# A chain of six transformer blocks on one core: value and output weights multiplied once, gates of all batches ahead of the loop, and a shifted residual moved tile by tile

## What is computed

```python
q = rms_norm(x @ Wq.T) * qk_gain ; k = rms_norm(x @ Wk.T) ; v = x @ Wv.T      # per head
g = sigmoid(x @ Wg.T + bg)                                  # per row and head
attn = softmax(where(mask, q @ k.T / sqrt(128), -inf))      # within a chunk of 64
y_in = attn @ v
gamma = exp(sum(log(g) over the chunk))
yc = q @ state ; state = state * gamma + k.T @ v            # from chunk to chunk
y = (y_in + yc) @ Wo.T
```

```python
def shift_token(t):
    t1, t2 = split(t, 2, axis=-1)
    t2 = pad(t2, ((0, 0), (1, 0), (0, 0)))[:, :-1]          # the row before
    return concatenate([t1, t2], axis=-1)
x = x + o @ wo
h = layer_norm(shift_token(x)) ; a, g = split(h @ w1 + b1, 2)
x = x + (a * gelu(g)) @ w2 + b2
```

## Time and profile before

| what | value |
|---|---|
| median of 3 runs | 2083.44 us (2080.21 to 2089.17) |
| profiled execution, its own time | 2075.68 us |
| its span | 2073.5 us |
| TensorE busy | 80% of the span |
| VectorE / ScalarE / GpSimd busy | 60% / 53% / 41% |
| mean granted TensorE clock | 0.899 |
| linear attention | 0 to 353 us |
| windows, first stage | 353 to 787 us |

### The profile page before, as it was taken

The page is one execution under the profiler, slowest core; times in us unless marked ns, Lnnn a source line. Parts: engine busy times, 40 slices in busy tenths (PEclk is TensorE's granted clock), DMA queues, the critical chain, the costliest instruction groups (busy, mean ns, idle before and its releaser), DMA issues. The chain is left out here.

```text
span 2073.5 us, 38265 instructions
## 1 busy us (share of the span) xinstructions
PE 1665.5 (80%) x13589; PEld 1193.2 (58%) x13589; DVE 1240.1 (60%) x3682; ACT 1090.7 (53%) x2758; POOL 854.6 (41%) x630
## 2 busy tenths in 40 slices
PE   6999998789998955888887789998856746858685
PEld 5888886466666633334544466666644535647464
DVE  2554543787777724555773787777726874545554
ACT  3656664677778722566543677888722102324232
POOL 1322322776666511223443866666504660321002
PEclk9999999999999986999876999999978877969888
DMA  4000000011111100000000111111100000000001
GB/s 193 1 1 1 1 1 1 22 29 30 24 28 29 27 5 1 1 1 2 1 2 1 27 24 29 25 29 31 25 6 0 1 1 0 21 21 1 1 6 56
DMA packets 31082, 36.55 MB, mean 18 GB/s; under 512 B 19120, under 2 KB 21168, under 8 KB 30512
## 3 DMA queue, kind: packets, MB, share of 16 engines
q1 hardware_dynamic: 29872, 32.01, 5.9%
q0 software_dynamic: 1024, 2.10, 0.3%
HBM read 12.08 MB, written 3.15 MB: 7 GB/s over the span
## 5 line engine op out<-in xcount | busy, mean ns | idle before, releaser
L965 ACT ACTIVATE arena<-ps 128x512 f32<-128x512 f32 (+4 forms) x702 | 377.1, 595 | 305.0 <-PE ps L321 122.8
L1200 ACT ACTIVATE arena<-ps 128x320 f32<-128x320 f32 (+4 forms) x256 | 132.2, 561 | 133.0 <-PE ps L679 130.6
L1100 ACT ACTIVATE arena<-arena,g_small 128x128 f32<-128x128 f32 x512 | 199.1, 404 | 0.5
L1550 DVE CUSTOM_DVE_ANT_0 arena<-ps,consts,g_ss 128x128 f32<-128x128 f32 x512 | 145.5, 346 | 78.9 <-PE ps L485 77.3
L321 PE MATMUL ps<-consts,arena 128*128 128x128 f32 x400 | 82.1, 351 | 136.8 <-DVE arena L1433 60.4
L2079 POOL TENSOR_TENSOR arena<-arena,consts 128x512 f32<-128x512 f32 (+1 forms) x64 | 93.5, 1461 | 191.2 <-ACT arena L1200 191.2
L2100 POOL TENSOR_TENSOR arena<-arena 128x512 f32<-128x512 f32 x64 | 82.2, 1284 | 181.7 <-DVE arena L1558 181.7
L321 PEld LDWEIGHTS ps<-consts,arena 128*128 128x128 f32 x400 | 57.8, 178 | 166.9 <-DVE arena L1433 65.4
L679 PE MATMUL ps<-arena 32*128 32x160 f32 (+4 forms) x1024 | 119.8, 461 | 21.3 <-ACT arena L1200 10.8
L1557 DVE TENSOR_TENSOR arena<-ps,tabs 128x512 f32<-128x512 f32 x128 | 87.6, 685 | 51.5 <-ACT arena L1069 44.8
L679 PEld LDWEIGHTS ps<-arena 32*128 32x128 f32 x1024 | 60.8, 210 | 87.4 <-ACT arena L1200 55.3
(11 more groups left out here) (253 smaller groups left out, 4262.3 us busy)
## 6 DMA issues: line engine op xcount, KB each, us to landing
arena<-arena SPq DMA_DIRECT2D x112, 128.0 KB, 2.3
weights<-in_w SPq DMA_DIRECT2D x1, 5069.0 KB, 24.2
weights<-in_w SPq DMA_DIRECT2D x1, 2052.0 KB, 12.7
arena<-Y SPq DMA_DIRECT2D x16, 128.0 KB
arena<-Y SPq DMA_DIRECT2D x16, 127.0 KB
consts<-in_c SPq DMA_DIRECT2D x1, 1278.0 KB, 8.8
out<-X SPq DMA_DIRECT2D x1, 1024.0 KB, 5.1
sorted_rows<-arena,e_idx POOLq DMA_INDIRECT x32
```

The costliest lines, as they stand in the source:

```text
L965: copy = lambda o, i: act.activation(o, i, ACT.Copy)
L1100: last = act.activation(g_p[:, n % 2, 4 * hf + i, :], g_sc[:, 4 * hf + i, :], ACT.Exp, scale=-1.0, bias=g_mn[:, h:h + 1], accum_out=g_rs[: ...
L1200: act.activation(b_p[:, U % 2, 2 * gp:2 * gp + 2, at:at + n], ps[:, b:b + 2, 0:n], ACT.Exp, scale=float(HD) ** -0.5).then_inc(s.b_exp, 1)
L1550: last = dve.tensor_tensor_reduce(g_sc[:, 4 * hf + i, :], ps[:, 4 + hf, i * P:(i + 1) * P], C("mask_f" if n % NT else "mask_f0"), g_ss[:, ...
```

## The change

It has four parts.

1. Since `(P v) Wo = P (x (Wv Wo))`, the value weights and output weights of each head are multiplied once (`fold_weights`, in two halves of four heads, by way of banks 3 and 4). `project_v` then makes values that already hold the output projection; `mix` is 10 matmuls of 128x128 with the probabilities stationary and adds up 8 heads in bank 6. `out_rows` and `keep_y` are gone, and `add_rows` reads bank 6.
2. `project_v` writes bank 7 and waits only for its own previous copy; `turn_q` waits for `a_kT` in place of `a_vin`.
3. x of all four batches is normalised and turned at the start; gates and decays are made once for all batches. The decay sums are three matmuls and six small adds on VectorE (`spans`), on which `turned_scores(0)` waits.
4. `shift` runs for each tile: two DMAs, and a third for the one row that passes to the next tile, behind `lookback` in SyncE's loop. 176 increments a group in place of 48 stand in the two waits on `gs.sh`.

```diff
+                def fold_weights(half):                      # TensorE
+                    for k in range(4):
+                        h = 4 * half + k
+                        last = tr(ps[:, 3, k * P:(k + 1) * P], W("a_qkv", 2048 + h * P, 2048 + (h + 1) * P), ident)
+                    last.then_inc(s.a_wT_ps, 1)
+                    pe.wait_ge(s.a_wT, half + 1)
+                    need(pe, s.a_vo, half)
+                    for k in range(4):
+                        h = 4 * half + k
+                        last = mm(ps[:, 4, k * P:(k + 1) * P], a_wT[:, k, :], W("a_wo", h * P, (h + 1) * P),
+                                  start=True, stop=True)
+                    last.then_inc(s.a_vo_ps, 1)
...
+                def gates():
+                    pe.wait_ge(s.a_xT, NB)
+                    for i in range(TT):
+                        last = mm(ps[:, 5, i * HA:(i + 1) * HA], a_xT[:, i // NT, i % NT * P:(i % NT + 1) * P], W("a_wg"),
...
+                def decays():
+                    pe.wait_ge(s.a_decay, 1)
+                    for k, name in enumerate(("half0", "ones", "cross")):
+                        last = mm(ps[:, 5, P * k + P:P * k + 2 * P], C(name), a_gate, start=True, stop=True)
                     last.then_inc(s.a_gsum, 1)
...
                 def project_v(n):
-                    need(pe, s.a_kT, n)
+                    need(pe, s.a_vin, n)
+                    pe.wait_ge(s.a_vo, h // 4 + 1)
                     for j in range(NT):
-                        last = mm(ps[:, 2, j * P:(j + 1) * P], a_xT[:, z % 2, j * P:(j + 1) * P],
-                                  W("a_qkv", 2048 + h * P, 2048 + (h + 1) * P), start=True, stop=True)
+                        last = mm(ps[:, 7, j * P:(j + 1) * P], a_xT[:, z, j * P:(j + 1) * P],
+                                  a_vo[:, h, :], start=True, stop=True)
...
                 def turned_scores(n):
                     need(pe, s.a_cross, n)
+                    if n == 0:
+                        pe.wait_ge(s.a_spans, 1)
...
                 def mix(n):
-                    need(pe, s.a_yT, n)
-                    pe.wait_ge(s.a_xT, begun(n, -4))
-                    pe.wait_ge(s.a_gate_in, begun(n, -3))
-                    pe.wait_ge(s.a_gamma, begun(n, -2))
-                    for i in range(NT):
-                        last = mm(ps[:, 6, i * P:], a_v[:, n % 4, i, :], a_mt[:, n % 2, i, 0:(NT - i) * P],
-                                  start=i == 0, stop=i == NT - 1, skip_group_check=True)
+                    if h == 0:
+                        need(pe, s.a_add, z)
+                    for i in range(NT):
+                        for j in range(i, NT):
+                            last = mm(ps[:, 6, j * P:(j + 1) * P], a_mt[:, n % 2, i, (j - i) * P:(j - i + 1) * P],
+                                      a_v[:, n % 4, i, :], start=h == i == j == 0, stop=h == HA - 1,
+                                      skip_group_check=True)
...
-                    if head(t - 1):
-                        out_rows(t - 1)
+                    if t == -4:
+                        turn_x(0)
+                    if t == -2:
+                        for z in range(1, NB):
+                            turn_x(z)
+                        gates()
+                    if -3 <= t < -1:
+                        fold_weights(t + 3)
                     if head(t + 2):
                         project_v(t + 2)
-                    if begins(t, -4):
-                        turn_x(t)
-                    if begins(t, -3):
-                        gates(t)
-                    if begins(t, -2):
-                        decays(t)
+                    if t == -1:
+                        decays()
```

ScalarE's loop, VectorE's start and its decay sums, and SyncE's loop:

```diff
                 for t in range(-4, HEADS + 1):               # ScalarE
-                    if begins(t, -1):
-                        decays(t)
+                    if t == -4:
+                        keep_x(0)
                     if head(t):
                         exps(t)
                         keep_raw(t)
-                    if head(t - 1):
-                        keep_y(t - 1)
                     if head(t + 1):
                         keep_q(t + 1)
+                    if t == -2:
+                        for z in range(1, NB):
+                            keep_x(z)
                     if head(t + 2):
                         squares(t + 2)
...
+                    if -3 <= t < -1:
+                        fold_weights(t + 3)
+                    if t == -2:
+                        log_gates()
...
+                    if t == -1:
+                        decays()
...
+                def spans():                                 # VectorE
+                    dve.wait_ge(s.a_gsum, 1)
+                    halves, tiles, over = (ps[:, 5, P * k:P * k + P].rearrange("p (z j h) -> p j z h", z=NB, j=NT)
+                                           for k in (1, 2, 3))
+                    after(dve.tensor_copy(a_dec[:, 0], over[:, 0:3]))
+                    tt(a_dec[:, 1], a_dec[:, 0], halves[:, 1:4], ALU.add)
...
+                for z in range(NB):
+                    variance(z)
+                for z in range(NB):
+                    norm_x(z)
...
+                def shift(n):                                # SyncE
+                    N, i, j = n0 + n, n % TT, n % NT
+                    sp.wait_ge(gs.add, N + 1)
+                    need(sp, gs.h2, m0 + n // NT)
+                    sp.dma_start(g_h[1:P, j, 64:128], Y[0:P - 1, i, 64:128]).then_inc(gs.sh, 16)
+                    sp.dma_start(g_h[:, j, 0:64], Y[:, i, 0:64]).then_inc(gs.sh, 16)
+                    if j < NT - 1:
+                        sp.dma_start(g_h[0:1, j + 1, 64:128], Y[P - 1:P, i, 64:128]).then_inc(gs.sh, 16)
...
-                    if at_step(t, 5):
-                        shift((t - 5) // 4)
                     if live(t + 2):
                         lookback(t + 2)
+                    if live(t - 2):
+                        shift(t - 2)
```

More of the change, by code:

```diff
@@ L366, in project_qk @@
                         for j in range(NT):
[L367 removed]
+                            last = mm(ps[:, c, j * P:(j + 1) * P], a_xT[:, z, j * P:(j + 1) * P],
                                       W("a_qkv", 1024 * c + h * P, 1024 * c + (h + 1) * P), start=True, stop=True)
@@ L967, in linear_attention, with keep_x, log_gates, decays @@
             def linear_attention():
-                def keep_x(t):
-                    z = (t + 4) // HA
+                def keep_x(z):
                     act.wait_ge(s.a_xT_ps, z + 1)
[L972 to L987, removed]
+                    copy(a_xT[:, z, :], ps[:, 7 - z % 2, :]).then_inc(s.a_xT, 1)
+                def log_gates():
+                    act.wait_ge(s.a_gate_in, 1)
+                    after(act.activation(a_gate, a_gate, ACT.Exp, scale=-1.0))
+                    act.activation(a_gate, a_gate, ACT.Ln, bias=1.0).then_inc(s.a_decay, 1)
+                def decays():
+                    act.wait_ge(s.a_spans, 1)
+                    for k, n in ((0, 3), (2, 2), (4, 1)):
+                        v = a_dec[:, k:k + 2, 0:n].rearrange("p k i z h -> p k (i z h)")
+                        last = act.activation(v, v, ACT.Exp, scale=-1.0)
+                    last.then_inc(s.a_gamma, 1)
                 def exps(n):
@@ L1438, in linear_attention, with variance @@
                 stream = lambda z: X[:, NT * z:NT * z + NT, :]
[L1440 to L1447 removed]
+                def variance(z):
+                    for i in range(NT * z, NT * z + NT):
+                        last = dve.bn_stats(stats[:, i, :], X[:, i, :])
+                    after(last)
+                    for i in range(NT * z, NT * z + NT):
+                        last = dve.bn_aggr(mv[:, i, :], stats[:, i, :])
+                    after(last)
+                    ts(rstd[:, NT * z:NT * z + NT], mv[:, NT * z:NT * z + NT, 1], EPS5, None, ALU.add).then_inc(gs.var, 1)
+                    rooted.next()
@@ new lines, in norm_x, with add_gate_bias @@
+                def norm_x(z):
+                    dve.wait_ge(gs.root4, z + 1)
+                    for i in range(NT * z, NT * z + NT):
+                        last = ts(Y[:, i, :], X[:, i, :], mv[:, i, 0:1], rstd[:, i:i + 1], ALU.subtract, ALU.mult)
+                    last.then_inc(gs.ln, 1)
+                def add_gate_bias():
+                    dve.wait_ge(s.a_gate_ps, 1)
+                    after(tt(a_gate.rearrange("p (i h) -> p i h", h=HA), ps[:, 5, 0:P].rearrange("p (i h) -> p i h", h=HA),
+                             wide(R("bg"), [P, TT, HA], 1), ALU.add))
+                    ts(a_gate, a_gate, -43.0, None, ALU.max).then_inc(s.a_gate_in, 1)
@@ L2032, in linear_attention @@
                 pool.wait_ge(s_loaded, 32)
-                for t in range(-6, HEADS):
+                for z in range(NB):
+                    root(z)
+                for t in range(-2, HEADS):
                     if head(t):
@@ L2310, in head @@
     return 0 <= n < HEADS
```

(8 more changed lines are left out.)

134 lines of the change are left out of this document (41 added, 93 removed).

## The result

The median of four runs after is 2049.98 us (2045.67 to 2055.11), that of four before 2082.05 us (2080.21 to 2089.17). The ratio is 0.9841, 95% interval 0.9808 to 0.9874: faster by 1.6%, some 32 us. I had forecast 2045 and faster; 2050 lies in the likeliest case's own range of 2036 to 2054. The profiled execution took 2050.73 us with a span of 2048.9, against 2075.68 and 2073.5 before, so between the two profiles the difference is only 24.6.

A forecast was written before the change was run, and what follows sets the result against it. TensorE's order was taken to bound linear attention's head step, and the last shift the windows' ends. Terms -19.2 - 10.2 - 0.2 - 1.9 + 5.5 - 12.6 = -38.6 us, from 2083.4 to 2045; range 2024 to 2063.

The forecast's parts named there:

- likeliest case: Whole kernel: the summed gains hold, 2045 us with its own range 2036 to 2054; chance 0.68.
- start, to scores(1): Start of linear attention: folding weights and all batches' work there delay scores(1) from 43.96 to 49.5, +5.5 us (+3.5 to +9).
- scores(1) to scores(31): Linear attention's loop: batch starts -19.2 us, 29 shorter head steps -10.2, step 30 -0.2.
- scores(31) to the last add: End of linear attention: without keep_y and out_rows the add begins at about 9.3 us instead of 11.16, -1.9 us.
- two windows stages: Windows stages' ends: tile-by-tile shift removes 6.3 of VectorE's 6.43 us idle, twice, -12.6 us.
- What bounds the step: Head step: TensorE's 9.33 us order, then ScalarE's chain ahead of scores at 8.99; 0.35 us a step, 10.2 in all.
- Batch starts: Linear attention's loop: three batch starts cost TensorE 19.2 us, which leave the path when gates and decays are made first.
- A: Head step: ScalarE's chain is shorter than read, TensorE bounds at 8.40 us; 17 us more gain, 2028; chance 0.06.
- B: Windows' ends: the small third DMA's 6.59 us are its own price, the wait stays; 2057 us; chance 0.08.
- C: Head step: stays at 9.3 us through the roots chain or an unseen handover; 2055 us; chance 0.08.
- D: Linear attention's loop: TensorE's idle drops its clock to 1.2 GHz; over 0.5% slower from 7 such steps; chance 0.04.
- E: Windows stages: SyncE becomes the bound at 9.0 us a step if small DMAs block it; 2050 to 2075; chance 0.06.

The follow-up runs named there:

- Experiment 3: The changed kernel with the copy keep_k moved from ScalarE to VectorE, ahead of its sums: 2027.51 us, ratio to before 0.9741.
- experiment 6: The kernel before with gates and decays made for batch 0 only, left out for batches 1 to 3: 2059.68 us in one execution.
- Experiment 4: The kernel before, shift still by groups, with its 127-partition DMA cut into 112 and 15: 2076.71 us, ratio to before 0.9985.

## Why the prediction was right, by its own steps

| term | predicted | measured |
|---|---|---|
| start, to scores(1) | +5.5 | +4.45 (48.41 against 43.96) |
| scores(1) to scores(31) | -29.6 | -26.83 (270.76 against 297.59) |
| scores(31) to the last add | -1.9 | -1.78 (9.38 against 11.16) |
| two windows stages | -12.6 | -14.5 (-8.1 and -6.4) |
| stages not touched | 0 | +14.1 |
| between the two profiles | -38.6 | -24.6 |

**What bounds the step.** Right: the order on TensorE had been the period, and with out_rows gone ScalarE's squares, keep_k and keep_probs were late next. Experiment 3 shows it by shortening that chain. The size was a little off. The term that was too small is the handover from the copy to scores, taken as 0.05 without a row for it and nearer 0.12: the copies begin at 165.10, two of them take 1.08 and so end at 166.18, and scores load at 166.30. The rest of the chain is as priced (project_qk 4.86 behind scores, squares 2.09 behind that). So the step is 9.07, not 8.99, and its gain 29 x 0.26 = 7.5 us instead of 10.2. That is nearly the whole miss of the second line; the rest is step 30, which took 7.78 (scores(30) load at 311.39) where 7.55 was forecast and 7.75 measured before. The mix, priced by project_qk's matmuls, took 2.23 (159.42 to 161.65) against 2.22.

**Batch starts.** Right, and priced by themselves in experiment 6. The step is 9.07 across them too.

**The start.** It came 1.05 us under the forecast, so that scores(1) lie at 48.41, just ahead of the 49 to 50 given as a sign. It ran partly at half clock, as I had assumed by taking the mean of both levels: tables by stretch give 0.57 from 30 to 38 us and 1.00 behind it. For 18 to 26 us they give 1.00 too, although the sixteen loads of project_qk(0) at 20.03 take 3.53 us as in the earlier trace rows, against 1.87 in the loop; these runs do not say why, so calling 0.22 a load the cold rate was not shown. The count of records was right: a transpose shows one (L381 x4 for four tiles) and a matmul two, other than the opening says. Linear attention is over at 329.7, where about 327 was forecast.

**The windows' end.** Right: the idle time is gone, not only most of it. The second stage gives 6.4 against the 433.9 of before (6.6 against the 434.1 of its other profiles), the term itself. The first gives more (8.1), and that stage lies anywhere between 431.1 and 436.0 in three profiles of the same kernel before, which is enough to account for it. My argument by the 15 ns a packet held: 127 packets crawl for 1.8 us in the DMA view after. Experiment 4 adds that the crawl belongs to the 127 partitions in one DMA, and not to the number or size of the packets, which are the same there. The table by stretch of before, in the middle of the crawl, has the 16 DMA engines busy for a share of 0.08 in the mean, little more than one of them:

```profile
752.00:754.00 2.00, 0.00 (x0) 0.00 (x0) 0.00 (x0) 0.00 (x0) 0.00 (x0) 1.00 0.08 18
```

 The Trainium skill, "DMA: Bandwidth & Descriptors", section "Why a DMA increments its semaphore by 16 and not by 1", gives the rule: the largest number up to 16 that divides the outermost dimension, so 16 for 112 partitions, 15 for 15, and 1 for 127. The trace agrees, 142 to 222 GB/s against 14 to 19. The 2 us of fixed cost that I had weighed stand in that page's section "Anatomy of one DMA — SWDGE (gpsimd) path", for DMAs that GpSimd issues, and not in "Bandwidth". Here SyncE is held 0.63 and 0.87 us by the two issues of the last tile. From the first issue (723.64) to the first data there are some 1.2 us, to the last data 3.2 (726.8), and VectorE goes on at 727.27 without a wait. So whatever is fixed lies beside VectorE's work, and the end of the data is known to VectorE within 0.5 us, the lower end of what I had allowed.

**Rivals.** A (8.40 a step) needed a shorter ScalarE chain; at 8.58 experiment 3 comes near it, by an edit that the change does not have. B and C are out by experiment 4 and by the step of 9.07. D, the clock falling in the loop because of 0.6 us idle in each step: the clock is 1.00. E, SyncE as the bound: its issues of L2278, L2279 and L2281 take 0.63, 0.85 and 0.59 in the middle of the stage (at 614.52), and none of them takes more than 1.88 in both stages. Before, the small third DMA held SyncE for 6.46 to 6.59 all sixteen times; it stood behind the 508-packet one.

**What I left out.** I costed the untouched stages at nothing and named no term for them. They took 14.1 us more than in the one profile of before that I had, 9.3 more than in another. The profile shown of before lay low among its own executions (2075.68 against a median of 2082), so a sum against it starts from the wrong side; I had scaled the result to the median of the runs, and this is why 2045 missed 2050 by 5 us and not by 13. It is in part luck. Against before's second profile, whose 2083.96 is near the median, linear attention gives 25.0 us (26.0 forecast), the windows 17.2 (12.6 forecast), and the untouched stages take back 9.3: the forecast came out near because a windows stage that happened to be long in that profile covers half of what I had left out. Whether the kernel after always carries those 9 us is open: two profiles of two do, and experiment 3, which holds the whole change but for one copy, does not.

## What to carry to other kernels

When work is taken off the engine that sets a loop's period, write down which engine is late next and by how much, and look at the order of its queue: here one copy moved to another engine shortened the step by 0.49 us, nearly twice what the removal of out_rows did (0.26). Price a wait at the end of a stage by the last transfer alone, and look at the number of partitions of each DMA before reorganising it: 127 crawls, 112 + 15 does not, though here that edit shortened the wait and not, measurably, the kernel. And read a second profile of the unchanged kernel before trusting a sum to a few microseconds, since stages that nobody touched moved by 5 to 14 us between profiles here, as much as the shift was worth.

## What the runs showed of the hardware

The granted clock behind the same stage start comes back at different times in the same kernel: TensorE was at 0.50 in the stretch from 30 to 40 us of small heads in one execution and at 0.90 in another, and the stage took 344.1 or 339.3 us; with experiment 4's 348.8 the three lengths lie 4.7 us apart. The ten profiles give no fourth length. The Trainium skill, "TensorE: Matmul & The Clock Gate", section "What's actually happening", says that the chip's watch over TensorE's activity runs freely and does not begin anew with the kernel, so that the moment at which a kernel's first matmuls speed up varies by half a microsecond either way. No run here shows that watch itself. What is measured here is another rise, in the middle of a kernel behind scattered work, and it varies by 11.7 us between executions of one kernel (31.9 and 43.6 us into the stage); for this the measurement decides.

A small DMA held SyncE's queue for 6.59 us behind one of 508 packets that moved at 14 to 19 GB/s; behind the same packets cut into two DMAs that moved at 142 GB/s and more it held it 0.75 us.

Idle time of 0.58 us ahead of each scores, in a step of 9.07 us, left the granted clock at 1.00 through the loop of the kernel after.
